# Feed-forward stage: the last layer norm's blocks normalised by ACT with a scale and a shift, the last three blocks added by DVE from PSUM, the last block a store of its own

## The chip, the cores and the metric

The kernel runs on one core of a Trainium2 chip. The metric is the device time of one launch in microseconds. Engines are named as in the profile: PE (TensorE matmuls), PEld (its weight loads), DVE (VectorE), ACT (ScalarE), POOL (GpSimd), SP (SyncE, which issues the DMAs here).

## The reference

Input x is 64 x 64 x 256, so 4096 tokens of 256. Self-attention, cross-attention and a feed-forward part follow one another, each added to x and followed by a layer norm. The change touches the third line only:

```python
def _layernorm(x, axis=-1, eps=1e-05):
    m = jnp.mean(x, axis=axis, keepdims=True)
    v = jnp.var(x, axis=axis, keepdims=True)
    return (x - m) / jnp.sqrt(v + eps)
...
def bitlinear(x, w):
    return jnp.einsum('bsi,oi->bso', _quant_act(x), _quant_weight(w))
gate = jax.nn.sigmoid(bitlinear(x, w_gate))
up = bitlinear(x, w_up)
h = gate * up
return bitlinear(h, w_down)
...
x = _layernorm(x + _L0_attn_ref(x, ...), axis=-1)
x = _layernorm(x + _L0_xattn_ref(x, ctx_2048, ...), axis=-1)
x = _layernorm(x + _L0_ffn_ref(x, L0_ffn_w_gate, L0_ffn_w_up, L0_ffn_w_down), axis=-1)
```

`_quant_act` divides a token's row by its largest magnitude over 127 and rounds; the weights are rounded to -1, 0 and 1 times a scale. The feed-forward width is 1024.

## The kernel before

`build` runs three parts in turn; `feed_forward` is the last. Its first half (lines up to 1116) quantises weights and activations. Its second half is one `nc.Block` in which every engine runs its own instruction list, written out in full without a hardware loop, and semaphores alone tie the lists together. Each engine executes its list strictly in order, so the order in the code is the order on the engine.

The tokens are cut into NB = 32 blocks of 128 rows; X holds all of them in SBUF, 256 columns of f32 for each block. `blocks(slot, lags)` calls `slot(n, has)` for n = 0, 1, 2 ... and `has(k)` says whether block n - k exists. In slot n the engines do, in this order:

- PE: gP(n) and uP(n) (each 4 matmuls of 512 columns, two PSUM banks); dP(n-3), the down projection, 8 matmuls of 256 columns into one of two banks dP0, dP1; hmP(n-2), 8 transposes of hm. gP(n) waits until ACT has read gP(n-1), uP(n) until DVE has read uP(n-1).
- ACT: sig(n), the sigmoid of gP; ds(n-3), dP times its scale; hqT(n-2), which takes the transposed hm from PSUM as bf16.
- DVE: hs(n) = uP times sig; its row maximum and the scales hsc, hinv, dsc; for block n-3 the row statistics (bn_stats at line 1256, bn_aggr at line 1258) of X, which wait for POOL's sum.
- POOL: the sum X = ds + X of block n-3 (line 1212); hm(n) (line 1216), the quantised hs(n), which waits for hinv(n); every fourth slot `roots`, for a group of four blocks: variance + eps (line 1203), then the power -0.5 (line 1205), both on 128 x 4; and the normalise of block n-7 (line 1146), (x - mean) * rstd in place. The roots of group m fall in slot 4m + 7, so in slots 7, 11, ... 31; those of the last group in slot 35.
- SP: one store of four blocks (512 KB) when their normalises are done.

POOL normalises blocks 0 to 27 and DVE, at its end, blocks 28 to 31. Slots 32 to 35 have no sig, hs or hm any more; they are the tail. In the text hs(27) is hs of block 27, and so for the other names.

Of the kernel before, what the change touches and what calls it, by code (L numbers as in the profile page):

```python
# [5 lines left out]
F32 = mybir.dt.float32  # L6
BF16 = mybir.dt.bfloat16
I32 = mybir.dt.int32
ACT = mybir.ActivationFunctionType
AX = mybir.AxisListType.X  # L10

P = 128
B, T, C = 64, 64, 256
# [7 lines left out]
NB = TOK // P  # L21
# [17 lines left out]
def wait(eng, sem, count):  # L39

    if not isinstance(count, int) or count > 0:
        eng.wait_ge(sem, count)
# [486 lines left out]
class Norm:  # L529
# [27 lines left out]
    def roots(self, act):  # L557

        act.wait_ge(self.s_small, 6)
        self.nc.scalar.activation(self.rstd[:, :], self.var[:, :], ACT.Ln, bias=self.eps_col[:, :]).then_inc(self.s_ln, 1)  # L560
        act.wait_ge(self.s_ln, 1)
        self.nc.scalar.activation(self.rstd[:, :], self.rstd[:, :], ACT.Exp, scale=-0.5).then_inc(self.s_rstd, 1)
# [461 lines left out]
def feed_forward(nc, a, X, norm, eps_col, ident, late, out, sem, sb, part):  # L1024
# [100 lines left out]
    hsc, hinv, dsc = sb("hsc", [P, NB], F32), sb("hinv", [P, NB], F32), sb("dsc", [P, NB], F32)  # L1125
    gP, uP, tP = (part.enter_context(nc.psum_tensor(n, [P, DFF], F32)) for n in ("gP", "uP", "hmP"))
    dP = [part.enter_context(nc.psum_tensor(n, [P, TILE], F32)) for n in ("dP0", "dP1")]
    s_g, s_u, s_t, s_dn = (sem("f_" + n) for n in ("g", "u", "t", "dn"))
# [1 line left out]
        "sig", "h", "max", "sc", "inv", "dsc", "hm", "te", "ds", "y"))  # L1130
    s_stats, s_mom, s_rstd, s_normed, s_out = (sem("f_" + n) for n in ("stats", "mom", "rstd", "normed", "out"))
    GROUP = 4
    NG = NB // GROUP
    moments = sb("ln3_moments", [P, NB, 2], F32)
    rstd, power = sb("ln3_rstd", [P, NB], F32), sb("ln3_power", [P, GROUP], F32)
    s_eps, s_power = sem("f_eps"), sem("f_power")

    def blocks(slot, lags):

        for n in range(NB + lags):  # L1140
            slot(n, lambda lag: 0 <= n - lag < NB)

    def normalise(eng, i):

        x = X[:, i, :]
        return eng.tensor_scalar(x, x, moments[:, i, 0:1], rstd[:, i:i + 1], ALU.subtract, ALU.mult)  # L1146

    with nc.Block() as block:  # L1148
        @block.tensor
        def _(pe):  # L1150
            def slot(n, has):
                if has(0):
                    for w, dst, free, ready in ((wg, gP, s_sig, s_g), (wu, uP, s_h, s_u)):
                        wait(pe, free, n)
                        for f in range(DFF // TILE):
                            for c in range(CC):
                                last = nc.tensor.matmul(dst[:, f * TILE:(f + 1) * TILE], xqT[:, c, n * P:(n + 1) * P], w[:, c, f * TILE:(f + 1) * TILE],  # L1157
                                                        start=(c == 0), stop=(c == CC - 1))
                        last.then_inc(ready, 1)
                if has(3):  # L1160
                    e = n - 3
                    wait(pe, s_te, e + 1)
                    wait(pe, s_ds, e - 1)
                    for f in range(FC):
                        last = nc.tensor.matmul(dP[e % 2][:, 0:C], hqT[:, e % 2, f * P:(f + 1) * P], wd[:, f, :], start=(f == 0), stop=(f == FC - 1))
                    last.then_inc(s_dn, 1)
                if has(2):
                    e = n - 2
                    wait(pe, s_hm, e + 1)
                    wait(pe, s_te, e)  # L1170
                    for f in range(FC):
                        last = nc.tensor.transpose(tP[:, f * P:(f + 1) * P], hm[:, e % 2, f * P:(f + 1) * P], ident[:, :])
                    last.then_inc(s_t, 1)

            blocks(slot, 3)

        @block.scalar
        def _(act):
            def slot(n, has):
                if has(0):  # L1180
                    wait(act, s_g, n + 1)
                    wait(act, s_h, n - 1)
                    nc.scalar.activation(sig[:, n % 2, :], gP[:, :], ACT.Sigmoid, scale=gsc[:, n:n + 1]).then_inc(s_sig, 1)
                if has(3):
                    e = n - 3
                    wait(act, s_dn, e + 1)
                    wait(act, s_dsc, e + 1)
                    wait(act, s_y, e - 1)
                    nc.scalar.activation(ds[:, e % 2, :], dP[e % 2][:, 0:C], ACT.Copy, scale=dsc[:, e:e + 1]).then_inc(s_ds, 1)
                if has(2):  # L1190
                    e = n - 2
                    wait(act, s_t, e + 1)
                    wait(act, s_dn, e - 1)
                    nc.scalar.activation(hqT[:, e % 2, :], tP[:, :], ACT.Copy, bias=-MAGIC).then_inc(s_te, 1)

            blocks(slot, 3)

        @block.gpsimd
        def _(pool):
            def roots(m):  # L1200
                own = slice(m * GROUP, (m + 1) * GROUP)
                wait(pool, s_mom, (m + 1) * GROUP)
                nc.gpsimd.tensor_scalar(rstd[:, own], moments[:, own, 1], EPS, None, ALU.add).then_inc(s_eps, 1)  # L1203
                wait(pool, s_eps, m + 1)
                nc.gpsimd.tensor_tensor(rstd[:, own], rstd[:, own], power[:, :], ALU.pow).then_inc(s_rstd, 1)  # L1205

            def slot(n, has):
                if has(3):
                    e = n - 3
                    wait(pool, s_ds, e + 1)  # L1210
                    x = X[:, e, :]
                    nc.gpsimd.tensor_tensor(x, ds[:, e % 2, :], x, ALU.add).then_inc(s_y, 1)  # L1212
                if has(0):
                    wait(pool, s_inv, n + 1)
                    wait(pool, s_t, n - 1)
                    nc.gpsimd.tensor_scalar(hm[:, n % 2, :], hs[:, n % 2, :], hinv[:, n:n + 1], MAGIC, ALU.mult, ALU.add).then_inc(s_hm, 1)  # L1216
                if has(4) and (n - 4) % GROUP == GROUP - 1:
                    roots((n - 4) // GROUP)
                if has(7) and n - 7 < NB - GROUP:
                    e = n - 7  # L1220
                    wait(pool, s_rstd, e // GROUP + 1)
                    normalise(nc.gpsimd, e).then_inc(s_normed, 1)

            nc.gpsimd.memset(power[:, :], -0.5).then_inc(s_power, 1)
            pool.wait_ge(s_power, 1)
            blocks(slot, 4)

        @block.sync
        def _(sp):
            dst = out.rearrange("(n p) c -> p n c", p=P)  # L1230
            for m in range(NG):
                own = slice(m * GROUP, (m + 1) * GROUP)
                sp.wait_ge(s_normed, (m + 1) * GROUP)
                sp.dma_start(dst[:, own, :], X[:, own, :]).then_inc(s_out, 16)
            sp.wait_ge(s_out, 16 * NG)

        @block.vector
        def _(dve):
            def slot(n, has):
                if has(0):  # L1240
                    wait(dve, s_sig, n + 1)
                    wait(dve, s_u, n + 1)
                    wait(dve, s_hm, n - 1)
                    nc.vector.scalar_tensor_tensor(hs[:, n % 2, :], uP[:, :], usc[:, n:n + 1], sig[:, n % 2, :],  # L1244
                                                   ALU.mult, ALU.mult).then_inc(s_h, 1)
                    wait(dve, s_h, n + 1)
                    nc.vector.tensor_reduce(hsc[:, n:n + 1], hs[:, n % 2, :], AX, ALU.max, apply_absolute_value=True).then_inc(s_max, 1)  # L1247
                    wait(dve, s_max, n + 1)
                    nc.vector.tensor_scalar(hsc[:, n:n + 1], hsc[:, n:n + 1], EPS, 1.0 / 127.0, ALU.max, ALU.mult).then_inc(s_sc, 1)  # L1249
                    wait(dve, s_sc, n + 1)  # L1250
                    nc.vector.reciprocal(hinv[:, n:n + 1], hsc[:, n:n + 1]).then_inc(s_inv, 1)  # L1251
                    nc.vector.tensor_scalar(dsc[:, n:n + 1], hsc[:, n:n + 1], wsc[:, 2:3], None, ALU.mult).then_inc(s_dsc, 1)  # L1252
                if has(3):
                    e = n - 3
                    wait(dve, s_y, e + 1)
                    nc.vector.bn_stats(stats[:, e, :], X[:, e, :]).then_inc(s_stats, 1)  # L1256
                    wait(dve, s_stats, e + 1)
                    nc.vector.bn_aggr(moments[:, e, :], stats[:, e, :]).then_inc(s_mom, 1)  # L1258

            blocks(slot, 3)  # L1260
            dve.wait_ge(s_rstd, NG)
            for i in range(NB - GROUP, NB):
                normalise(nc.vector, i).then_inc(s_normed, 1)


def constants():
# [48 lines left out]
```

## Time and profile before

| | us |
|---|---|
| median of the 3 runs | 1627.86 (1627.15 to 1629.86) |
| the profiled execution | 1630.34 |
| its span, first to last instruction | 1628.5 |
| second half of the feed-forward stage, in the span | about 1492 to 1628.5 |

Over the whole span PE is busy 91%, DVE 81%, ACT 82% and POOL 76% of the time, but these are averages over three very different parts. In the last stage the shares must be read from the stage itself. The profile lists instructions with start and duration, and names behind "<-" the instruction whose semaphore ended an engine's idle time. An instruction's own duration may overlap the next one's on the same engine by some hundredths of a microsecond.

### The profile page before, as it was taken

To read this page: it belongs to the slowest core of one execution; us is meant where nothing else is said; L and a number is where in the kernel's file an instruction comes from. 1 tells how busy PE (TensorE), PEld (TensorE's weight loads), DVE (VectorE), ACT (ScalarE), POOL (GpSimd) and SP (SyncE) were. 2 spreads that over 40 slices of the span, in tenths; PEclk is the share of its full clock that TensorE was granted. 3 is DMA by queue.
4 is the path that set the end of the run, shared out by engine and by line. 5 is a ranking of instruction groups with operands and counts; after the bars stand their busy time and mean duration, and the time that the engine had idled before them with its cause. 6 is when DMAs were issued, how large, how long until landed. Compare 5 with 4: busy or idle time off the path is not lost. (4 is left out here: it accounts for less than half of the span.)

```text
span 1628.5 us, 54216 instructions
## 1 busy us (share of the span) xinstructions
PE 1487.4 (91%) x20018; PEld 1083.8 (67%) x20018; DVE 1322.9 (81%) x2913; ACT 1334.4 (82%) x4174; POOL 1231.7 (76%) x1147
## 2 busy tenths in 40 slices
PE   6998999999999999999999968799999999845996
PEld 3666777777777777777777755366666666633664
DVE  3887777777777777777777778699999999967986
ACT  5877888888888888888888856599999999976664
POOL 5999888888898898898898846466666666611787
PEclk9999999999999999999999978999999999976999
DMA  6700000000000000000000002200000000000011
GB/s 222 191 2 15 16 3 15 16 15 3 15 15 3 16 15 5 13 15 15 3 15 3 3 2 68 86 3 2 0 0 0 0 0 0 0 1 0 14 39 53
DMA packets 27066, 36.92 MB, mean 23 GB/s; under 512 B 8288, under 2 KB 19872, under 8 KB 26848
## 3 DMA queue, kind: packets, MB, share of 16 engines
q1 hardware_dynamic: 26848, 33.99, 6.6%
q8 instruction: 140, 2.29, 0.5%
q14 instruction: 78, 0.64, 0.1%
HBM read 29.79 MB, written 4.19 MB: 21 GB/s over the span
## 5 line engine op out<-in xcount | busy, mean ns | idle before, releaser
L420 DVE SCALAR_TENSOR_TENSOR X<-projP,r,X 128x256 f32<-128x256 f32 x512 | 211.3, 476 | 2.5 <-PE projP L254 2.4
L234 PEld LDWEIGHTS svP<-W,xT 128*128 128x128 bf16 x3072 | 182.7, 98 | 31.4 <-issue 1.4
L205 PE MATMUL qkssP<-xT,W 128*128 128x512 bf16 x768 | 190.4, 384 | 13.5 <-POOL W L485 11.1
L480 POOL TENSOR_TENSOR y_sql<-y_sq 128x512 bf16<-128x512 f32 x128 | 133.0, 1039 | 80.5 <-ACT y_sq L321 80.1
L234 PE MATMUL svP<-W,xT 128*128 128x128 bf16 x3072 | 192.9, 219 | 0.7 <-issue 0.7
L205 PE MATMUL kP<-xT,W 128*128 128x512 bf16 x768 | 188.4, 382 | 0.0
L254 PE MATMUL projP<-W,y 128*128 128x256 bf16 x1024 | 177.1, 275 | 3.2 <-POOL yl L480 3.2
L943 ACT ACTIVATE x_probs<-x_scores,x_ntop 128x64 f32<-128x64 f32 x512 | 170.0, 335 | 7.4 <-DVE x_ntop L985 7.4
L336 ACT ACTIVATE probs<-scores,ntop 128x64 f32<-128x64 f32 x512 | 170.5, 339 | 1.9 <-DVE ntop L410 1.9
L1008 POOL TENSOR_TENSOR x_probs<-x_probs,x_inv 128x512 f32<-128x512 f32 x64 | 66.7, 1042 | 107.9 <-DVE x_inv L968 107.9
L480 POOL TENSOR_TENSOR k_sql<-k_sq 128x512 bf16<-128x512 f32 x128 | 133.1, 1040 | 19.8 <-ACT k_sq L341 19.2
L254 PE MATMUL projP<-W,yl 128*128 128x256 bf16 x512 | 140.9, 275 | 0.0
L889 PE MATMUL xq<-qc,WQ 128*128 128x512 bf16 x576 | 136.5, 383 | 3.8 <-PEq L661 2.9
L514 POOL TENSOR_TENSOR ql<-q 128x512 bf16<-128x512 f32 x128 | 139.0, 1086 | 0.0
L480 POOL TENSOR_TENSOR q_sql<-q_sq 128x512 bf16<-128x512 f32 x128 | 133.0, 1039 | 7.6 <-ACT q_sq L328 7.6
L205 PEld LDWEIGHTS kP<-xT,W 128*128 128x128 bf16 x768 | 75.7, 99 | 92.2 <-issue 2.8
L517 POOL TENSOR_TENSOR vl<-v 128x512 bf16<-128x512 f32 x128 | 135.7, 1060 | 0.0
L480 POOL TENSOR_TENSOR yl<-y 128x512 bf16<-128x512 f32 x128 | 133.0, 1039 | 0.0
L450 DVE TENSOR_TENSOR ptl<-pyP,pth 128x256 bf16<-128x256 f32 x128 | 54.3, 424 | 96.8 <-ACT pth L355 96.8
L997 DVE TENSOR_TENSOR qh<-turn 64x512 f32<-64x512 f32 x128 | 128.6, 1005 | 3.1
L1019 POOL TENSOR_TENSOR qhl<-qh 128x1024 bf16<-128x1024 f32 x64 | 121.1, 1893 | 6.2 <-DVE qh L997 6.2
L433 DVE COPY v<-svP 128x512 f32<-128x512 f32 x128 | 88.4, 691 | 44.9 <-PE svP L234 44.1
(190 smaller groups left out, 4829.1 us busy)
## 6 DMA issues: line engine op xcount, KB each, us to landing
w_stage<-in_wqkvp SPq DMA_DIRECT2D x16, 512.0 KB, 3.5
x_stage<-in_xT SPq DMA_DIRECT2D x8, 512.0 KB, 3.6
X<-in_x SPq DMA_DIRECT2D x1, 4096.0 KB, 17.2
x_stage<-in_ctxT SPq DMA_DIRECT2D x8, 512.0 KB, 3.6
out<-X SPq DMA_DIRECT2D x8, 512.0 KB, 2.9
okv<-in_L_xattn_W_o SPq DMA_DIRECT2D x1, 2048.0 KB, 11.7
okv<-in_wgT SPq DMA_DIRECT2D x1, 1024.0 KB, 4.9
okv<-in_wuT SPq DMA_DIRECT2D x1, 1024.0 KB, 7.2
```

What stands on the lines that cost most here:

```text
L205: last = nc.tensor.matmul(dst[:, :], weight(parity, u, i, c), xT[:, z, c, tok], start=(c == 0 and k == 0), stop=(c == CC - 1 and k == 2))
L234: last = nc.tensor.matmul(svP[:, b * D:(b + 1) * D], xT[:, u, c, t * TILE + b * P:t * TILE + (b + 1) * P], weight(parity, z, 2, c), start= ...
L254: last = nc.tensor.matmul(projP[:, b * C:(b + 1) * C], y_part, W[:, (j - 3) // NT % 2, z, 3 * CC * D:], start=(i == 0), stop=(i == 2))
L336: last = nc.scalar.activation(probs[:, b, :], scores[:, b, :], ACT.Exp, bias=ntop[:, b:b + 1], accum_out=total[:, b:b + 1])
L420: last = nc.vector.scalar_tensor_tensor(acc, projP[:, b * C:(b + 1) * C], r[:, PB + b:PB + b + 1], acc, ALU.mult, ALU.add)
L480: return nc.gpsimd.tensor_tensor(dst[:, :], src[:, :], high(src, slice(None), 0, TILE), ALU.subtract)
L514: nc.gpsimd.tensor_tensor(ql[:, j % 2, :], q[:, j % 2, :], high_of(q, j % 2), ALU.subtract).then_inc(s_ql, 1)
L517: nc.gpsimd.tensor_tensor(vl[:, j % 4, :], v[:, j % 4, :], high_of(v, j % 4), ALU.subtract).then_inc(s_vl, 1)
L889: last = nc.tensor.matmul(qP[k][:, :], at(WQ[:, u, :, k], g), qc[:, z, j * TILE:(j + 1) * TILE], start=(i == 0), stop=(i == 2))
L943: last = nc.scalar.activation(probs[:, s, b, :], scores[:, b, :], ACT.Exp, bias=ntop[:, b:b + 1], accum_out=total[:, b:b + 1])
L997: last = nc.vector.tensor_tensor(qh[KVC:P, j % 2, :, i, :], turn[rows, 0], turn[rows, 1], ALU.add)
L1019: nc.gpsimd.tensor_tensor(qhl[:, s, :], flat, flat.bitcast(BF16)[:, 1::2], ALU.subtract).then_inc(s_ql, 1)
```

## The change

ACT normalises blocks 0 to 27 in place of POOL, as Identity(x * rstd + shift) with shift = -mean * rstd; block n-8 is done in slot n, behind hqT(n-2). POOL's `roots` computes shift for these seven groups with two more instructions. Blocks from LATE = 29 on are summed by DVE directly from PSUM, X = dP * dsc + X, so ACT's ds and POOL's sum are left out for them. The last group of four is split in a group of three (28 to 30) and one of one (31), each with roots and a store of its own; DVE normalises them as before. PE's wait before dP follows the new readers of dP. Stores of the first 28 blocks wait for ACT.

```diff
     GROUP = 4
-    NG = NB // GROUP
+    groups = [slice(i, i + GROUP) for i in range(0, NB - GROUP, GROUP)] + [slice(NB - GROUP, NB - 1), slice(NB - 1, NB)]
+    NG, MAIN, LATE = len(groups), NB - GROUP, NB - 3
...
 (PE)
-                    wait(pe, s_ds, e - 1)
+                    wait(pe, s_ds, min(e - 1, LATE))
+                    wait(pe, s_y, e - 1 if e - 2 >= LATE else 0)
...
 (ACT)
-                if has(3):
+                if has(3) and n - 3 < LATE:
                     e = n - 3
...
-            blocks(slot, 3)
+                if has(8) and n - 8 < MAIN:
+                    e = n - 8
+                    x = X[:, e, :]
+                    wait(act, s_shift, e // GROUP + 1)
+                    nc.scalar.activation(x, x, ACT.Identity, bias=shift[:, e:e + 1], scale=rstd[:, e:e + 1]).then_inc(s_by_act, 1)
+
+            blocks(slot, 4)
...
 (POOL)
             def roots(m):
-                own = slice(m * GROUP, (m + 1) * GROUP)
-                wait(pool, s_mom, (m + 1) * GROUP)
+                own = groups[m]
+                wait(pool, s_mom, own.stop)
                 nc.gpsimd.tensor_scalar(rstd[:, own], moments[:, own, 1], EPS, None, ALU.add).then_inc(s_eps, 1)
                 wait(pool, s_eps, m + 1)
-                nc.gpsimd.tensor_tensor(rstd[:, own], rstd[:, own], power[:, :], ALU.pow).then_inc(s_rstd, 1)
+                nc.gpsimd.tensor_tensor(rstd[:, own], rstd[:, own], power[:, 0:own.stop - own.start], ALU.pow).then_inc(s_rstd, 1)
+                if own.stop <= MAIN:
+                    nc.gpsimd.tensor_scalar(shift[:, own], moments[:, own, 0], -1.0, None, ALU.mult).then_inc(s_neg, 1)
+                    wait(pool, s_neg, m + 1)
+                    wait(pool, s_rstd, m + 1)
+                    nc.gpsimd.tensor_tensor(shift[:, own], shift[:, own], rstd[:, own], ALU.mult).then_inc(s_shift, 1)
...
-                if has(4) and (n - 4) % GROUP == GROUP - 1:
-                    roots((n - 4) // GROUP)
-                if has(7) and n - 7 < NB - GROUP:
-                    e = n - 7
-                    wait(pool, s_rstd, e // GROUP + 1)
-                    normalise(nc.gpsimd, e).then_inc(s_normed, 1)
+                for m in range(NG):
+                    if n - 4 == groups[m].stop - 1:
+                        roots(m)
...
 (DVE)
                 if has(3):
                     e = n - 3
+                    if e >= LATE:
+                        x = X[:, e, :]
+                        wait(dve, s_dn, e + 1)
+                        wait(dve, s_dsc, e + 1)
+                        wait(dve, s_y, e)
+                        nc.vector.scalar_tensor_tensor(x, dP[e % 2][:, 0:C], dsc[:, e:e + 1], x, ALU.mult, ALU.add).then_inc(s_y, 1)
                     wait(dve, s_y, e + 1)
                     nc.vector.bn_stats(stats[:, e, :], X[:, e, :]).then_inc(s_stats, 1)
```

On POOL, from the roots in slot 27 to hm in slot 28. Before:

```order
L1203 TENSOR_SCALAR ln3_rstd<-ln3_moments 128x4 [waits f_mom]
L1205 TENSOR_TENSOR ln3_rstd<-ln3_rstd,ln3_power 128x4 [waits f_eps]
L1146 TENSOR_SCALAR X<-X,ln3_moments,ln3_rstd 128x256 [waits f_rstd]
L1212 TENSOR_TENSOR X<-ds,X 128x256 [waits f_ds]
L1216 TENSOR_SCALAR hm<-hs,hinv 128x1024 [waits f_t,f_inv]
```

After:

```order
L1206 TENSOR_SCALAR ln3_rstd<-ln3_moments 128x4 [waits f_mom]
L1208 TENSOR_TENSOR ln3_rstd<-ln3_rstd,ln3_power 128x4 [waits f_eps]
L1210 TENSOR_SCALAR ln3_shift<-ln3_moments 128x4
L1213 TENSOR_TENSOR ln3_shift<-ln3_shift,ln3_rstd 128x4 [waits f_rstd,f_neg]
L1220 TENSOR_TENSOR X<-ds,X 128x256 [waits f_ds]
L1224 TENSOR_SCALAR hm<-hs,hinv 128x1024 [waits f_t,f_inv]
```

The normalise between the roots and the next sum is gone; two instructions on 128 x 4 stand in its place.

On ACT, slot 28 and the start of slot 29: sig(28), ds(25), hqT(26), sig(29), ds(26). Before:

```order
L1183 ACTIVATE sig<-gP,gsc 128x1024 [waits f_h,f_g]
L1189 ACTIVATE ds<-dP1,dsc 128x256 [waits f_y,f_dsc,f_dn]
L1194 ACTIVATE hqT<-hmP 128x1024 [waits f_dn,f_t]
L1183 ACTIVATE sig<-gP,gsc 128x1024 [waits f_h,f_g]
L1189 ACTIVATE ds<-dP0,dsc 128x256 [waits f_y,f_dsc,f_dn]
```

After:

```order
L1181 ACTIVATE sig<-gP,gsc 128x1024 [waits f_h,f_g]
L1187 ACTIVATE ds<-dP1,dsc 128x256 [waits f_y,f_dsc,f_dn]
L1192 ACTIVATE hqT<-hmP 128x1024 [waits f_dn,f_t]
L1197 ACTIVATE X<-X,ln3_shift,ln3_rstd 128x256 [waits f_shift]
L1181 ACTIVATE sig<-gP,gsc 128x1024 [waits f_h,f_g]
L1187 ACTIVATE ds<-dP0,dsc 128x256 [waits f_y,f_dsc,f_dn]
```

A normalise with a wait for shift stands between hqT and the next block's sig.

On DVE, the end of its list, from the statistics of block 31. Before:

```order
L1256 BN_STATS ln3_stats<-X 128x6 [waits f_y]
L1258 BN_AGGR ln3_moments<-ln3_stats 128x2 [waits f_stats]
L1146 TENSOR_SCALAR X<-X,ln3_moments,ln3_rstd 128x256 [waits f_rstd]
L1146 TENSOR_SCALAR X<-X,ln3_moments,ln3_rstd 128x256 x3
L1148 UNCONDITIONAL_BRANCH
```

After:

```order
L1267 SCALAR_TENSOR_TENSOR X<-dP1,dsc,X 128x256 [waits f_y,f_dsc,f_dn]
L1269 BN_STATS ln3_stats<-X 128x6 [waits f_y]
L1271 BN_AGGR ln3_moments<-ln3_stats 128x2 [waits f_stats]
L1279 TENSOR_SCALAR X<-X,ln3_moments,ln3_rstd 128x256 [waits f_rstd]
L1279 TENSOR_SCALAR X<-X,ln3_moments,ln3_rstd 128x256 x2
L1279 TENSOR_SCALAR X<-X,ln3_moments,ln3_rstd 128x256 [waits f_rstd]
```

DVE makes the sum of block 31 itself, and the wait for the last roots stands before its last normalise alone.

## Rows read from the trace of the kernel before

**Rows 1.** Who waited for instructions on ds, last stage: us, times.

```profile
  DVE ln_stats L1256: 13.1, 9
```

**Rows 2.** Timeline: start, us, engine, line, operation; DVE and POOL, blocks 27 to 29.

```profile
1594.61 1.28 DVE L1244 SCALAR_TENSOR_TENSOR hs<-uP,usc,sig 128x1024 f32<-128x1024 f32 x1
...
1597.37 0.16 DVE L1251 RECIPROCAL hinv<-hsc 128x1 f32<-128x1 f32 x1
...
1597.64 1.12 POOL L1216 TENSOR_SCALAR hm<-hs,hinv 128x1024 f32<-128x1024 f32 x1 [0.50 <-DVE hinv L1251]
...
1598.13 1.28 DVE L1244 SCALAR_TENSOR_TENSOR hs<-uP,usc,sig 128x1024 f32<-128x1024 f32 x1
...
1598.85 0.23 POOL L1203 TENSOR_SCALAR ln_rstd<-ln_moments 128x4 f32<-128x4 f32 x1
1599.16 1.04 POOL L1205 TENSOR_TENSOR ln_rstd<-ln_rstd,ln_power 128x4 f32<-128x4 f32 x1
...
1600.31 1.22 POOL L1146 TENSOR_SCALAR X<-X,ln_moments,ln_rstd 128x256 f32<-128x256 f32 x1
...
1601.50 0.73 POOL L1212 TENSOR_TENSOR X<-ds,X 128x256 f32<-128x256 f32 x1
...
1602.26 0.43 DVE L1256 BATCH_NORM_STATS2 ln_stats<-X 128x6 f32<-128x256 f32 x1 [1.10 <-POOL X L1212]
...
1602.83 1.28 DVE L1244 SCALAR_TENSOR_TENSOR hs<-uP,usc,sig 128x1024 f32<-128x1024 f32 x1
```

**Rows 3.** Timeline of the same stretch, PE and ACT: hmP(27), ds(25), hqT(26), sig(29).

```profile
1597.70 1.04 PE L1172 MATMUL hmP<-ident,hm 128*128 128x128 f32 x8
1597.90 0.47 ACT L1189 ACTIVATE ds<-dP,dsc 128x256 f32<-128x256 f32 x1 [0.61 <-PE dP L1165]
...
1598.78 1.02 ACT L1194 ACTIVATE hqT<-hmP 128x1024 bf16<-128x1024 f32 x1 [0.40 <-PE hmP L1172]
...
1599.70 1.11 ACT L1183 ACTIVATE sig<-gP,gsc 128x1024 f32<-128x1024 f32 x1
```

**Rows 4.** Timeline of the tail, from hm(31) to the last normalises.

```profile
1612.88 1.12 POOL L1216 TENSOR_SCALAR hm<-hs,hinv 128x1024 f32<-128x1024 f32 x1 [0.50 <-DVE hinv L1251]
...
1616.58 1.02 ACT L1194 ACTIVATE hqT<-hmP 128x1024 bf16<-128x1024 f32 x1 [0.40 <-PE hmP L1172]
...
1617.49 0.43 DVE L1256 BATCH_NORM_STATS2 ln_stats<-X 128x6 f32<-128x256 f32 x1 [4.04 <-POOL X L1212]
...
1617.65 1.05 PE L1165 MATMUL dP<-wd,hqT 128*128 128x256 bf16 x8 [1.11 <-ACT hqT L1194]
...
1621.23 1.22 POOL L1146 TENSOR_SCALAR X<-X,ln_moments,ln_rstd 128x256 f32<-128x256 f32 x1
1621.28 0.43 DVE L1256 BATCH_NORM_STATS2 ln_stats<-X 128x6 f32<-128x256 f32 x1 [1.25 <-POOL X L1212]
1621.74 0.18 DVE L1258 BATCH_NORM_AGGREGATE ln_moments<-ln_stats 128x2 f32<-128x6 f32 x1
...
1622.73 1.04 POOL L1205 TENSOR_TENSOR ln_rstd<-ln_rstd,ln_power 128x4 f32<-128x4 f32 x1
1623.80 1.38 DVE L1146 TENSOR_SCALAR X<-X,ln_moments,ln_rstd 128x256 f32<-128x256 f32 x4 [1.89 <-POOL ln_rstd L1205]
```

**Rows 5.** Groups of instructions over the whole span: busy us, mean ns, then idle before.

```profile
L420 DVE SCALAR_TENSOR_TENSOR X<-projP,r,X 128x256 f32<-128x256 f32 x512 | 211.3, 476 | 2.5 <-PE projP L254 2.4
...
L1063 ACT ACTIVATE xs<-X,magic,xinv 128x256 f32<-128x256 f32 x32 | 16.6, 588 | 5.1 <-DVE xinv L1091 5.1
...
L1055 ACT ACT_TABLE_LOAD x1 | 1.3, 1283 | 0.0
...
L813 POOL TENSOR_TENSOR kvw<-kvf,kvw 128x128 bf16<-128x128 f32 x1 | 0.5, 473 | 0.0
```

**Rows 6.** DMA issues: count, KB each, median us from issue to landing.

```profile
out<-X SPq DMA_DIRECT2D x8, 512.0 KB, 2.9
...
tabs<-in_rope SPq DMA_DIRECT2D x1, 96.0 KB, 2.1
```

More of the change, by code:

```diff
@@ L1132, in feed_forward @@
     GROUP = 4
-    NG = NB // GROUP
+    groups = [slice(i, i + GROUP) for i in range(0, NB - GROUP, GROUP)] + [slice(NB - GROUP, NB - 1), slice(NB - 1, NB)]
+    NG, MAIN, LATE = len(groups), NB - GROUP, NB - 3
     moments = sb("ln3_moments", [P, NB, 2], F32)
-    rstd, power = sb("ln3_rstd", [P, NB], F32), sb("ln3_power", [P, GROUP], F32)
-    s_eps, s_power = sem("f_eps"), sem("f_power")
+    rstd, shift, power = sb("ln3_rstd", [P, NB], F32), sb("ln3_shift", [P, NB], F32), sb("ln3_power", [P, GROUP], F32)
+    s_eps, s_power, s_neg, s_shift = sem("f_eps"), sem("f_power"), sem("f_neg"), sem("f_shift")
+    s_by_act = sem("f_byact")
     def blocks(slot, lags):
@@ L1141, in blocks @@
             slot(n, lambda lag: 0 <= n - lag < NB)
-    def normalise(eng, i):
-        x = X[:, i, :]
-        return eng.tensor_scalar(x, x, moments[:, i, 0:1], rstd[:, i:i + 1], ALU.subtract, ALU.mult)
     with nc.Block() as block:
@@ L1200, in roots @@
             def roots(m):
-                own = slice(m * GROUP, (m + 1) * GROUP)
-                wait(pool, s_mom, (m + 1) * GROUP)
+                own = groups[m]
+                wait(pool, s_mom, own.stop)
                 nc.gpsimd.tensor_scalar(rstd[:, own], moments[:, own, 1], EPS, None, ALU.add).then_inc(s_eps, 1)
                 wait(pool, s_eps, m + 1)
-                nc.gpsimd.tensor_tensor(rstd[:, own], rstd[:, own], power[:, :], ALU.pow).then_inc(s_rstd, 1)
+                nc.gpsimd.tensor_tensor(rstd[:, own], rstd[:, own], power[:, 0:own.stop - own.start], ALU.pow).then_inc(s_rstd, 1)
[4 more added lines that the diff above has]
+                    nc.gpsimd.tensor_tensor(shift[:, own], shift[:, own], rstd[:, own], ALU.mult).then_inc(s_shift, 1)
             def slot(n, has):
-                if has(3):
+                if has(3) and n - 3 < LATE:
                     e = n - 3
@@ L1230, in _ @@
             dst = out.rearrange("(n p) c -> p n c", p=P)
-            for m in range(NG):
-                own = slice(m * GROUP, (m + 1) * GROUP)
-                sp.wait_ge(s_normed, (m + 1) * GROUP)
+            for own in groups:
+                if own.stop <= MAIN:
+                    sp.wait_ge(s_by_act, own.stop)
+                else:
+                    sp.wait_ge(s_normed, own.stop - MAIN)
                 sp.dma_start(dst[:, own, :], X[:, own, :]).then_inc(s_out, 16)
@@ L1260, in _ @@
             blocks(slot, 3)
-            dve.wait_ge(s_rstd, NG)
-            for i in range(NB - GROUP, NB):
-                normalise(nc.vector, i).then_inc(s_normed, 1)
+            for m in (NG - 2, NG - 1):
+                own = groups[m]
+                dve.wait_ge(s_rstd, m + 1)
+                for i in range(own.start, own.stop):
+                    x = X[:, i, :]
+                    nc.vector.tensor_scalar(x, x, moments[:, i, 0:1], rstd[:, i:i + 1], ALU.subtract, ALU.mult).then_inc(s_normed, 1)
 def constants():
```

## Prediction, made before the changed kernel was run

> **What bounds the kernel now.** I read four views of the profile, in this order: what the row statistics wait for, the instructions of one group of four blocks in order of time, the same for the last microseconds, and the prices of like operations. Only the last stage matters: it is the only one the change touches.
>
> Call slot n the one in which DVE makes hs(n). In a plain slot DVE is never idle: hs(27) starts at 1594.61 and hs(28) at 1598.13, 3.52 us later [rows 2], with the block's maximum, scales and row statistics between them. In one slot of four it stops. POOL finishes hm(27), then computes the roots (0.23, then the power, 1.04), then normalises a block (1.22), and only then adds block 25 (0.73), for whose sum DVE's statistics have waited 1.10 us. So hs(29) starts at 1602.83, 4.70 us after hs(28) [rows 2]. DVE's statistics wait nine times and 13.1 us in all [rows 1]. Three of these waits lie in the tail (4.04, and twice 1.25, [rows 4]); the other 6.6 us are six waits of 1.1, one for each of the roots in slots 7, 11, ... 27. Since DVE has no slack in a plain slot, each is paid in full: 4.70 - 3.52 = 1.18 us.
>
> The tail is bound elsewhere. TensorE ends dP(31) at 1618.70, but POOL is busy with an add and a normalise for each leftover block; it starts the last normalise at 1621.23, the last power ends at 1623.77, and DVE then normalises four blocks to 1625.18 [rows 4]. The 512 KB store of these four lands 2.9 us later [rows 6], and the span ends at 1628.5: 3.32 us after the last normalise.
>
> **The six groups.** POOL loses its 28 normalises of 1.22 and gains, per group, a negation and a product on 128x4. The negation is of the form of the 0.233 us step in [rows 2]. A product of 128x4 is not in the trace. The nearest rows: two tensor-tensor operations, 473 ns at 128 elements [rows 5] and 0.73 us at 256 [rows 2], whose straight line gives 0.23 at four; and the power on the same 128x4, 1.04. I take 0.23, since a product is like the plain operations and not like a power; 1.04 stays as the upper bound.
>
> ACT gains 24 normalises inside its loop (and four in the tail). The row with the same form, f32 128x256 from SBUF with a bias and a scale per partition, is 588 ns [rows 5]. In a plain slot this hides. After hs(27), with start t = 1594.61: the transposes hmP start at t + 3.09 and end at t + 4.13, hqT runs from t + 4.17 to t + 5.19 [rows 3]; consecutive ACT instructions overlap by 0.10 (hqT ends at 1599.80, sig starts at 1599.70). So the normalise starts at t + 5.09 and sig(29) at t + 5.58; it ends 1.11 later, at t + 6.69, and hs(29) is due at t + 7.03. The cover is 0.34 less a handover, which I take as 0.06 (between 0.03, power to DVE at the end, and 0.11, hinv to hm, [rows 2, 4]): **0.28 us of slack**. If that cover were gone, each 0.1 of excess would cost 0.05 a slot, because the loop spans two slots. ACT's 0.47 us ds [rows 3] starts when dP ends, so it is not pushed.
>
> In the slot after the roots it does not hide. ACT takes its instructions in order, and the normalise of the new group's first block now stands ahead of sig(29) and waits for shift. In the times of rows 2 and 3: the power ends at 1600.20; negation to 1600.43; product (0.08 later, as between the 128x4 step and the power) 1600.51 to 1600.74; normalise(20) on ACT 1600.80 to 1601.39, though ACT was free at 1599.80; sig(29) 1601.29 to 1602.40; hs(29) at 1602.46. It was 1602.83, and undisturbed it would be 1598.13 + 3.52 = 1601.65. So the stall shrinks only from 1.18 to 0.81: **0.37 us a group, 2.2 us for six**. The old wait, by itself, would shrink more: the add of block 25 runs from 1600.77 to 1601.50 and the statistics start at 1601.53 and not 1602.26, 0.73 earlier. ACT's wait is what comes in its place and ends last. Behind it are queued sig(29), for which DVE waits, and with it gP of block 30 on TensorE. gP(30) needs the PSUM that sig(29) reads and moves with it; uP(30) waits for the end of hs(29) anyway, and TensorE is not asked for hs(30) before that, so nothing is added.
>
> **The tail**, in the times of before. hm(31) still starts at 1612.88. Its roots give shift 3.10 later (1600.74 - 1597.64), at 1615.98; normalise(24) runs on ACT from 1616.04 to 1616.63, and hqT(31), which starts at 1616.58 now [rows 4], can start 0.10 before that ends. A tie: no cost, but no cover either. dP(31) ends at 1618.70 as before. ACT's ds and POOL's add for blocks 29 to 31 are gone; DVE's one operation from PSUM has the form of the 476 ns row [rows 5]: 1618.74 to 1619.22. Statistics 1619.25, aggregation 0.46 later (1621.28 to 1621.74, [rows 4]) and ended at 1619.89. POOL is idle: first step at 1620.00, power at 1620.31 to 1621.35 (I take 1.04 for one element as for four). DVE has by then normalised blocks 28 to 30, whose roots needed dP(30) only; the last block takes 0.41 (1.38 for four back to back is 0.345 each, a lone one is a little longer): 1621.38 to 1621.79, against 1625.18. **3.4 us.**
>
> The last store is 128 KB and not 512. The nearest row is a 96 KB transfer landing in 2.1 us, against 2.9 [rows 6]. I take 2.1, so the span ends 2.5 and not 3.3 us after the normalise: **0.8 us**, between 0 (no gain by size) and 1.1. The 384 KB store ahead of it on SP's queue is issued at about 1621.0 and would be nearly through.
>
> The Trainium skill, "DMA: Bandwidth & Descriptors", section on the anatomy of one DMA, gives about 2.0 us plus bytes over 436 GB/s. By it, as an estimate, the last store would take 2.3 us in place of 3.2, a gain of 0.9 and not 0.8. Its figure for 512 KB is 0.3 above this trace's 2.9, so the row decides, and the sum moves by 0.1 us.
>
> Sum: 2.2 + 3.4 + 0.8 = 6.4 us. The profiled execution took 1630.34 with a span of 1628.5, so it would become 1623.9 with a span of 1622.1. It lay 2.5 us above the median of the runs shown. From that median, 1627.86, the forecast is **1621.5 us**.
>
> **Rivals.**
>
> *ACT's wait hides.* If shift came earlier than I think or sig had more room, each group would gain the 0.73 of POOL's path: 4.4 in place of 2.2, and 1619.3 us. Against it: ACT is free at 1599.80 and shift can't be there before the power ends at 1600.20. For it: only the overlap assumptions at each handover. 12%.
>
> *The product costs what the power costs.* With 1.04 us in place of 0.23 each group stalls 1.62 and not 0.81, a loss of 0.44 a group against now, 2.6 for six; the same 0.8 then holds hqT(31) in the tail, 4.2 less 0.8 is 3.4. Net gain 0.8 us: 1627.1. For it: all other small POOL tensor-tensor rows here are this power. 13%.
>
> *The last store or the last roots give nothing.* The tail gains only 3.4 or less (store lands in 2.9, or a wait on the small roots), total about 5: 1622.9. 15%.
>
> *Slower: ACT becomes the bound.* One mechanism, in its loop hqT, normalise, sig: if the normalise took more than 0.59 + 0.28 = 0.87 us, plain slots would lengthen too. Up to there 0.1 us costs 0.7 (six groups and the tail), so 6.4 falls to 4.4; beyond it 1.6 per 0.1 (18 plain slots by 0.05 more). Break-even is at 1.15 us, 3.3 us slower at 1.35. At POOL's price for this very operation, 1.22 [rows 2], it gives 1.2 us slower, 1629.1; at 1.5, about 1633.5. For it: ACT's added work is the only one in every slot, and the operands are its own output area, f32 in place. Against: the 588 ns row has the same shape and operands. Nor is a table exchanged: the 588 ns operations run behind the load at L1055 [rows 5], and Sigmoid after them without another. 5% in all, most of it at or above 1.2.
>
> *The forecast*: 55%.
>
> **Numbers.** A measurement of this kernel can tell some 0.2%, 3.3 us, from no change. The forecast, the hidden wait and the weak store are all faster by more than that: 82%. The slow product, and milder cases of ACT's, lie within it: 14%. Slower: 4%. The range covers the hidden wait (1619.3 less the spread of the base, about 1) and reaches up to 1625.3, past the point (1624.3) where a product with half the extra would land; left out are the slow product in full and ACT's case, some 18%.
>
> **What would show it.** Right: hs starts 3.52 apart in three slots and about 4.3 in the fourth; ahead of ACT's normalise, once in four, an idle time of about 1.0 us ended by POOL's product; DVE's statistics waiting some 0.4 in that slot, with the rest of the stall ahead of hs and ended by sig; ACT's normalise near 590 ns; POOL's product near 230 ns; from the end of dP(31) to the end of the last normalise 3.1 us, where it was 6.5; three stores in the last nine microseconds, the last landing in 2.1. Wrong: hs waiting for sig in plain slots (ACT's loop is too long), hqT(31) waiting behind normalise(24) (shift late), or the last power starting later than 2 us after dP(31).

## The result, and the profile after

| | before | after |
|---|---|---|
| median, us (11 runs each) | 1628.44 | 1623.43 |
| ratio, 95% interval | | 0.9963 (0.9950 to 0.9976) |
| span of the profiled execution | 1628.5 | 1618.4 |
| hs(0) to hs(31) in the profile | 114.34 | 112.19 |
| hs(31) to the end of the span | 18.65 | 14.35 |

The ratio is worth 6.0 us, at a forecast of 6.4 (1621.5 from 1627.86, a ratio of 0.9961); its interval spans 3.9 to 8.1 us, so the whole times alone don't tell the forecast from a gain of 5. The median after, 1623.43, lies 1.9 above the 1621.5 and below the 1625.3 up to which the forecast reached; that of before is itself 0.6 above the 1627.86 that the forecast started from. The two spans differ by 10.1 us, which is more than the change did: 3.65 of it had arisen before hs(0), in stages that are the same in both kernels. The two distances in the last rows of the table leave that out, and all runs below are read by them. They give 2.15 + 4.30 = 6.45 us. One row of each kernel carries the start of both:

```profile
L1244 DVE SCALAR_TENSOR_TENSOR hs<-uP,usc,sig x32: 1273/1284/1286, 1495.5 to 1609.9; 128x1024 f32<-128x1024 f32 x32
```

is hs before (shortest, median and longest duration in ns, then the first and the last start), and after the change:

```profile
L1251 DVE SCALAR_TENSOR_TENSOR hs<-uP,usc,sig x32: 1273/1284/1286, 1491.9 to 1604.0; 128x1024 f32<-128x1024 f32 x32
```

The slot after the roots, as [rows 2] and [rows 3] showed it before: timeline of the changed kernel (start, us, engine, line, operation, and the idle time before it with what ended it).

```profile
1592.19 1.12 POOL L1224 TENSOR_SCALAR hm<-hs,hinv 128x1024 f32<-128x1024 f32 x1 [1.71 <-DVE hinv L1258]
...
1592.68 1.28 DVE L1251 SCALAR_TENSOR_TENSOR hs<-uP,usc,sig 128x1024 f32<-128x1024 f32 x1
...
1593.71 1.03 POOL L1208 TENSOR_TENSOR ln_rstd<-ln_rstd,ln_power 128x4 f32<-128x4 f32 x1
...
1594.83 0.24 POOL L1210 TENSOR_SCALAR ln_shift<-ln_moments 128x4 f32<-128x4 f32 x1
...
1595.15 0.20 POOL L1213 TENSOR_TENSOR ln_shift<-ln_shift,ln_rstd 128x4 f32<-128x4 f32 x1
...
1595.39 0.60 ACT L1197 ACTIVATE X<-X,ln_shift,ln_rstd 128x256 f32<-128x256 f32 x1 [1.03 <-POOL ln_shift L1213]
...
1595.89 1.09 ACT L1181 ACTIVATE sig<-gP,gsc 128x1024 f32<-128x1024 f32 x1
...
1596.07 0.43 DVE L1269 BATCH_NORM_STATS2 ln_stats<-X 128x6 f32<-128x256 f32 x1 [0.35 <-POOL X L1220]
...
1597.02 1.28 DVE L1251 SCALAR_TENSOR_TENSOR hs<-uP,usc,sig 128x1024 f32<-128x1024 f32 x1 [0.31 <-ACT sig L1181]
```

hs(28) to hs(29) is 4.34 us, where it was 4.70. DVE waits twice: 0.35 for POOL's sum, then 0.31 for sig, which stands on ACT behind a normalise that waited 1.03 for shift. The rest of the 0.83 by which this pitch exceeds the plain 3.51 is overlap lost at the two waits: in a plain slot the statistics and hs each start some 0.08 before the instruction ahead of them has ended. POOL, without its normalise, now waits 1.7 us for hinv in a plain slot (first row), where it waited 0.50. The waits of the whole stage, us in total, times and longest:

```profile
ACT X L1197 <- POOL ln_shift L1213: 7.4, 7, 1.5
...
DVE ln_stats L1269 <- POOL X L1220: 2.1, 6, 0.4
DVE hs L1251 <- ACT sig L1181: 1.9, 6, 0.3
```

Before, [rows 1] had one line of 13.1 us in their place, of which 6.6 lay in the six groups. The tail, for [rows 4]:

```profile
1610.26 0.60 ACT L1197 ACTIVATE X<-X,ln_shift,ln_rstd 128x256 f32<-128x256 f32 x1 [1.50 <-POOL ln_shift L1213]
...
1610.77 1.02 ACT L1192 ACTIVATE hqT<-hmP 128x1024 bf16<-128x1024 f32 x1
...
1611.85 1.05 PE L1163 MATMUL dP<-wd,hqT 128*128 128x256 bf16 x8 [1.11 <-ACT hqT L1192]
1612.93 0.48 DVE L1267 SCALAR_TENSOR_TENSOR X<-dP,dsc,X 128x256 f32<-128x256 f32 x1 [1.87 <-PE dP L1163]
1613.45 0.43 DVE L1269 BATCH_NORM_STATS2 ln_stats<-X 128x6 f32<-128x256 f32 x1
...
1614.01 1.58 DVE L1279 TENSOR_SCALAR X<-X,ln_moments,ln_rstd 128x256 f32<-128x256 f32 x4
...
1614.57 0.58 POOL L1208 TENSOR_TENSOR ln_rstd<-ln_rstd,ln_power 128x1 f32<-128x1 f32 x1
```

From the start of dP(31) to the last normalise's end (1614.01 + 1.58 = 1615.59) it takes 3.74 us; before, 1617.65 to 1625.18, it took 7.53. The last stores, for [rows 6] (count, KB, us to landing):

```profile
out<-X SPq DMA_DIRECT2D x7, 512.0 KB, 2.9
out<-X SPq DMA_DIRECT2D x1, 384.0 KB, 2.5
out<-X SPq DMA_DIRECT2D x1, 128.0 KB, 2.4
```

### The profile page after: what moved, and what is told of

Its sections match the earlier page's. It is cut to its first block and busy times, and to the rows that moved or that the text cites. A ratio compares the mean times of both kernels' runs of the same rounds, so it can differ in the third digit from the quotient of the medians.

```text
span 1618.4 us, 54034 instructions
## 1 busy us (share of the span) xinstructions
PE 1459.8 (90%) x19815; PEld 1082.1 (67%) x20018; DVE 1322.4 (82%) x2916; ACT 1345.4 (83%) x4199; POOL 1201.4 (74%) x1132
## 5 line engine op out<-in xcount | busy, mean ns | idle before, releaser
L205 PE MATMUL qkssP<-xT,W 128*128 128x512 bf16 x641 | 161.3, 382 | 33.5 <-issue 20.3
L889 PE MATMUL xq<-qc,WQ 128*128 128x512 bf16 x514 | 123.0, 382 | 7.4 <-PEq L661 3.1
```

The lines of the kernel that those rows point to most:

```text
L205: last = nc.tensor.matmul(dst[:, :], weight(parity, u, i, c), xT[:, z, c, tok], start=(c == 0 and k == 0), stop=(c == CC - 1 and k == 2))
L889: last = nc.tensor.matmul(qP[k][:, :], at(WQ[:, u, :, k], g), qc[:, z, j * TILE:(j + 1) * TILE], start=(i == 0), stop=(i == 2))
```

## The experiments

Every kernel is the changed one with the edit shown. "First" is hs(0) to hs(31), "tail" is hs(31) to the end of the span, both in us and from one profiled execution of each kernel; kernels that don't differ in the first distance repeat it to 0.05 us (112.19 to 112.24). Each ratio is taken against runs of the kernel before from the same series. The last three kernels ran once.

| kernel | first | tail | ratio to before (95%) |
|---|---|---|---|
| before | 114.34 | 18.65 | |
| after | 112.19 | 14.35 | 0.9963 (0.9950 to 0.9976) |
| ACT's normalise only | 112.24 | 17.45 | 0.9963 (0.9943 to 0.9984) |
| new tail only | 114.44 | 16.59 | 0.9970 (0.9951 to 0.9988) |
| ACT's normalise one slot later | 109.89 | 14.54 | 0.9939 (0.9922 to 0.9956) |
| roots one slot later | 116.52 | 14.32 | 0.9982 (0.9962 to 1.0002) |
| second power | 118.11 | 15.30 | 1.0006 (0.9991 to 1.0021) |
| roots ahead of hm | 107.26 | 14.29 | 0.9933 (0.9908 to 0.9958) |
| POOL normalises, roots ahead of hm | 110.52 | 16.20 | 0.9967 (0.9943 to 0.9991) |
| one last store | 112.21 | 16.21 | one run |
| no sums on DVE | 112.19 | 16.45 | one run |
| the same, roots of 28 to 30 first | 112.21 | 15.94 | one run |

### The two halves of the change

New tail only: POOL normalises as before.

```diff
 (ACT)
-                if has(8) and n - 8 < MAIN:
-                    e = n - 8
-                    ...
-            blocks(slot, 4)
+            blocks(slot, 3)
 (POOL, behind the roots; no shift is computed)
+                if has(7) and n - 7 < MAIN:
+                    e = n - 7
+                    x = X[:, e, :]
+                    wait(pool, s_rstd, e // GROUP + 1)
+                    nc.gpsimd.tensor_scalar(x, x, moments[:, e, 0:1], rstd[:, e:e + 1], ALU.subtract, ALU.mult).then_inc(s_by_act, 1)
```

> The new tail alone: POOL normalises blocks 0 to 27 as before the change, with no shift, while DVE makes the last three sums and the last store is split. hs(0) to hs(31) as before the change, 114.3 us. Tail: if its 4.3 us came from the new sums and stores alone, 14.35; Theory A expects less, because POOL still has four normalises of 1.22 to do behind hm(31) and between the last two roots, so the last power ends about 1.8 us later than with ACT's normalise: about 16.0 to 16.3.

ACT's normalise only: one group of four at the end, no sums on DVE.

```diff
-    groups = [slice(i, i + GROUP) for i in range(0, NB - GROUP, GROUP)] + [slice(NB - GROUP, NB - 1), slice(NB - 1, NB)]
-    NG, MAIN, LATE = len(groups), NB - GROUP, NB - 3
+    groups = [slice(i, i + GROUP) for i in range(0, NB, GROUP)]
+    NG, MAIN, LATE = len(groups), NB - GROUP, NB
...
-            for m in (NG - 2, NG - 1):
+            for m in (NG - 1,):
```

> ACT's normalise alone; the last three blocks go through ACT and POOL as before the change, one group of four and one store at the end. hs(0) to hs(31) 112.2 us as after the change. Tail: ds(30) and hqT(31) stand behind the normalise that waits for shift (0.4 us), then ds 0.47 and POOL's sum 0.73, roots of four, four normalises and a 512 KB store: 18.65 - 1.2 = about 17.4 us. If taking the normalise off POOL did nothing for the tail: 18.65.

Measured: 114.44 and 16.59 for the new tail, 112.24 and 17.45 for ACT's normalise. So the 2.1 us of the first distance come from ACT's normalise alone. In the tail the parts give 2.06 and 1.20 each on its own, but 4.30 where both are made: they need each other. Without ACT's normalise POOL's four leftover normalises hold the last roots back; with POOL free, ACT's and POOL's detour for the last sums does (the run with no sums on DVE, below, has 16.45 where the change has 14.35). In the timeline of the new tail alone POOL is still at its last normalise when the sums are long done:

```profile
1616.00 3.64 POOL L1227 TENSOR_SCALAR X<-X,ln_moments,ln_rstd 128x256 f32<-128x256 f32 x3
...
1620.17 0.18 DVE L1271 BATCH_NORM_AGGREGATE ln_moments<-ln_stats 128x2 f32<-128x6 f32 x1
1620.81 1.27 POOL L1227 TENSOR_SCALAR X<-X,ln_moments,ln_rstd 128x256 f32<-128x256 f32 x1
...
1622.40 0.58 POOL L1203 TENSOR_TENSOR ln_rstd<-ln_rstd,ln_power 128x1 f32<-128x1 f32 x1
1623.02 0.41 DVE L1279 TENSOR_SCALAR X<-X,ln_moments,ln_rstd 128x256 f32<-128x256 f32 x1 [0.80 <-POOL ln_rstd L1203]
```

The excess over 16.0 to 16.3 is in the store: SP issues the last three within 1.4 us there (2.3 after the change), and the last one lands in 3.1 us and not 2.4.

### Which wait ends last in a group

Two waits stand in the slot after the roots, so two edits take one away each. ACT's normalise one slot later:

```diff
-                if has(8) and n - 8 < MAIN:
-                    e = n - 8
+                if has(9) and n - 9 < MAIN:
+                    e = n - 9
...
-            blocks(slot, 4)
+            blocks(slot, 5)
```

> ACT's normalise one slot later (block n-9). Two distances are read from the trace: from the start of hs(0) to the start of hs(31), 114.3 us before and 112.2 after the change, and from hs(31) to the end of the span, 18.65 and 14.35. Theory A (ACT's wait for shift ends last in each group): with the wait covered, the stall of a group falls from 0.82 to about 0.44, what POOL's late sum leaves, so the first distance becomes 109.9 us; DVE still waits 0.35 for POOL's sum, six times. Rival B (the stall is POOL's sum alone, ACT's wait lies beside it): 112.2, unchanged. Both expect the tail at about 14.4.

Roots one slot later, behind the sum, which frees the sum and delays shift:

```diff
+                for m in range(NG):
+                    if n - (5 if groups[m].stop <= MAIN else 4) == groups[m].stop - 1:
+                        roots(m)
                 if has(0):
                     wait(pool, s_inv, n + 1)
...
-                for m in range(NG):
-                    if n - 4 == groups[m].stop - 1:
-                        roots(m)
```

> The roots of the first seven groups run one slot later, behind the sum and ahead of hm. DVE's statistics then never wait for POOL's sum, but shift comes 0.73 us later for ACT. Theory A: the stall of a group grows from 0.82 to 1.55, hs(0) to hs(31) becomes 116.6 us, slower than before the change. Rival B (POOL's sum is the stall): the stall goes, 112.2 - 6 x 0.82 = 107.3 us. Tail unchanged for both, about 14.4.

Measured: 109.89 and 116.52 us, against 109.9 and 116.6 for theory A (ACT's wait for shift ends last). Its rival (POOL's sum alone) expected 112.2 and 107.3. With the normalise one slot later ACT's wait for shift is gone from the list and DVE's for the sum stays, at its old size (0.35 of a stall that is now 0.44):

```profile
DVE ln_stats L1269 <- POOL X L1220: 2.1, 6, 0.4
```

With the roots one slot later it is the other way round, and the remaining wait is the longer one:

```profile
ACT X L1197 <- POOL ln_shift L1213: 11.7, 7, 1.7
...
DVE hs L1251 <- ACT sig L1181: 8.9, 6, 1.6
```

### More of the same wait

A power more on 128x4, ahead of the negation; its result is overwritten:

```diff
                 if own.stop <= MAIN:
+                    nc.gpsimd.tensor_tensor(shift[:, own], moments[:, own, 1], power[:, :], ALU.pow).then_inc(s_spare, 1)
+                    wait(pool, s_spare, m + 1)
```

> A second power on 128x4, whose result is not used, stands ahead of the negation in the roots of the first seven groups: about 1.12 us later shift and sum. Theory A (ACT's wait on the path, nothing hides it): the stall of a group grows by the full 1.12, from 0.82 to 1.94; hs(0) to hs(31) 112.2 + 6.7 = 118.9 us; tail longer by 1.1, since norm(24) holds hqT(31): 15.5. If there was room beside the stall: less than 0.5 a group, under 115.

Measured: 118.11 and 15.30; each stall is 1.82 us, 0.99 longer than after the change. The extra power costs 1.00 and not 1.12, because it follows the first without a wait and starts as that one ends:

```profile
1597.38 1.03 POOL L1208 TENSOR_TENSOR ln_rstd<-ln_rstd,ln_power 128x4 f32<-128x4 f32 x1
...
1598.38 1.01 POOL L1210 TENSOR_TENSOR ln_shift<-ln_moments,ln_power 128x4 f32<-128x4 f32 x1
```

So what shift is late by is paid in full in the groups and nearly so in the tail (0.95 of 1.00), and the time is that of the kernel before (1.0006). This also prices the slow-product rival: a product of power's cost would have eaten nearly all of the gain.

### Taking both waits away

Roots in the same slot, behind the sum but ahead of hm:

```diff
+                for m in range(NG):
+                    if n - 4 == groups[m].stop - 1:
+                        roots(m)
                 if has(0):
                     wait(pool, s_inv, n + 1)
...
-                for m in range(NG):
-                    if n - 4 == groups[m].stop - 1:
-                        roots(m)
```

> The roots stay in their slot but run ahead of hm, behind the sum. Theory A: shift is ready before ACT asks for it and POOL's next sum is in time, so both waits of a group go; hs(0) to hs(31) 112.2 - 6 x 0.82 = 107.3 us, and no idle time of DVE in any slot after the first; hm of that slot comes about 0.4 us later, which nobody waits for. Rival C (a late hm is paid: DVE's scales or the transposes of hm wait for it): 0.4 us a group come back, 109.7 us or more. Tail 14.4 for both, with norm(24) no longer waiting. In all 4.9 us faster than after the change, about 0.66% faster than before it; by C 3.4 us or less.

Measured: 107.26 and 14.29, as theory A said, and a ratio of 0.9933. This is the fastest kernel here, 5.0 us below the change in the two distances together (4.93 + 0.06); the intervals of the two ratios overlap, so the distances decide. POOL had been idle 1.7 us in each slot, waiting for hinv; the roots now run in that time. In its timeline hm(27) starts without a wait at 1589.10, some 0.3 us late (hinv(27) ended at 1588.69, and in a plain slot hm follows it by 0.1), and nobody waits for it: its transposes run a slot later, at 1592.36.

```profile
1587.48 1.03 POOL L1208 TENSOR_TENSOR ln_rstd<-ln_rstd,ln_power 128x4 f32<-128x4 f32 x1
...
1588.92 0.20 POOL L1213 TENSOR_TENSOR ln_shift<-ln_shift,ln_rstd 128x4 f32<-128x4 f32 x1
...
1589.10 1.12 POOL L1227 TENSOR_SCALAR hm<-hs,hinv 128x1024 f32<-128x1024 f32 x1
1589.16 0.18 DVE L1271 BATCH_NORM_AGGREGATE ln_moments<-ln_stats 128x2 f32<-128x6 f32 x1
1589.27 1.28 DVE L1251 SCALAR_TENSOR_TENSOR hs<-uP,usc,sig 128x1024 f32<-128x1024 f32 x1
...
1592.36 1.04 PE L1170 MATMUL hmP<-ident,hm 128*128 128x128 f32 x8
```

Is ACT needed for that at all? POOL normalises as before the change, with the new tail, and the roots stand ahead of hm (the edit of "new tail only" and the one above, together):

> POOL still normalises blocks 0 to 27 (the new tail, no shift), but its roots run ahead of hm in their slot. If what cost the stall was the roots' place in POOL's list, moving them does part of the work without ACT: roots 1.36 from the end of the sum, hm 1.12, normalise 1.22, so the next sum ends about 0.6 late against 1.18 before: hs(0) to hs(31) 114.3 - 6 x 0.6 = 110.8 us, shorter than after the change (112.2). If POOL's load (sum, hm, normalise: 3.1 of each 3.5 us, plus 1.4 for four blocks) is the limit wherever the roots stand: 114.3, unchanged.

Measured: 110.52 us in the first distance, shorter than after the change (112.19), with no work moved to ACT. Five stalls of 0.67 remain, and none for the first group, whose roots meet a POOL that has no normalises yet:

```profile
DVE ln_stats L1269 <- POOL X L1215: 2.9, 5, 0.6
```

So the place of the roots cost more than the normalise did; but sum, hm and normalise take 3.07 us of a slot of 3.51, and the roots need 0.23 + 1.04 = 1.27 more in one slot, so a stall stays. The tail is 16.20, and first distance and tail add up to 126.72, against 126.54 after the change: beside the new tail, moving the roots alone comes within 0.2 us of moving the normalises alone. ACT's normalise is worth 110.52 - 107.26 = 3.26 us once the roots stand right, and 2.25 (114.44 - 112.19) where they stand wrong.

### The parts of the tail

One last store: the edits to `groups` and to DVE's last loop of "ACT's normalise only", with LATE kept.

> Only the split of the last group is undone: DVE still makes the last three sums, but roots for four blocks run after the last statistics, and one store of 512 KB ends the kernel. hs(0) to hs(31) unchanged, 112.2 us. Tail: the power on 128x4 instead of 128x1 (1.04 against 0.58, 0.46), four normalises instead of one behind it (1.38 against 0.40, about 1.0), and the larger store (3.3 against 2.8 to the end of the span, 0.5): 14.35 + 1.95 = 16.3 us. If the split was worth only the store: 14.9.

Measured: 16.21. The split is worth 1.86 us, most of it not the store itself but the roots and normalises behind the last statistics: the last normalise ends 12.90 us after hs(31) and not 11.54 (1.36), and from there to the end of the span it takes 3.31 and not 2.81 (0.50).

No sums on DVE:

```diff
-    NG, MAIN, LATE = len(groups), NB - GROUP, NB - 3
+    NG, MAIN, LATE = len(groups), NB - GROUP, NB
```

> Only DVE's sums from PSUM are undone: the last three blocks go through ACT's scaled copy and POOL's sum, with the split groups kept. hs(0) to hs(31) unchanged, 112.2 us. Tail: ds 0.47 and sum 0.73 with two handovers in place of 0.48 (0.8 us), and ds(30) now stands between norm(24), which waits for shift, and hqT(31) (about 0.4): 14.35 + 1.2 = 15.6 us. If ACT's order there cost nothing: 15.15.

Measured: 16.45, and the expectation missed by 0.85. Its timeline shows what it had left out:

```profile
1615.32 0.72 POOL L1220 TENSOR_TENSOR X<-ds,X 128x256 f32<-128x256 f32 x1 [1.80 <-ACT ds L1187]
...
1616.45 0.87 POOL L1208 TENSOR_TENSOR ln_rstd<-ln_rstd,ln_power 128x3 f32<-128x3 f32 x1
...
1617.31 0.23 POOL L1206 TENSOR_SCALAR ln_rstd<-ln_moments 128x1 f32<-128x1 f32 x1
1617.37 1.38 DVE L1279 TENSOR_SCALAR X<-X,ln_moments,ln_rstd 128x256 f32<-128x256 f32 x4 [0.64 <-POOL ln_rstd L1208]
```

The roots of blocks 28 to 30 stand on POOL behind the sum of block 31, which waits for the last ds, although their statistics were done 1.9 us earlier (1614.20). DVE's first three normalises wait for them, and so does the last root. With these roots moved ahead of that sum:

```diff
+                if n == NB + 2:
+                    roots(NG - 2)
                 if has(3) and n - 3 < LATE:
...
-                for m in range(NG):
+                for m in range(NG - 2):
                     if n - 4 == groups[m].stop - 1:
                         roots(m)
+                if n == NB + 3:
+                    roots(NG - 1)
```

> As the run without DVE's sums (tail 16.45 us, 0.85 over its expectation), with one step moved: in slot 34 POOL computes the roots of blocks 28 to 30 ahead of the sum of block 31. If the 0.85 was POOL's order (these roots behind that sum, the last roots behind both, and DVE's four normalises behind the first): tail about 15.6 us. If it was something in ACT's or DVE's sums themselves: 16.4, unchanged. hs(0) to hs(31) 112.2 for both.

Measured: 15.94, so 0.51 of the 0.85 was that order. From hs(31) to the last normalise's end it is now 12.82 us (1605.67 to 1618.49), 1.28 more than after the change (1604.05 to 1615.59, 11.54): the 1.2 expected. The other 0.3 lie behind that end, 3.11 us to the end of the span against 2.81. They are not in the last store, which lands in 2.4 us in both. SP's last two waits in this run are

```profile
SPq L1145 <- DMA out<-X: 2.0, 1, 2.0
SPq L1145 <- PEq L1145: 0.5, 1, 0.5
```

The first, for the last landing, is 2.0 us after the change too; the second is 0.2 there:

```profile
SPq L1145 <- PEq L1145: 0.2, 1, 0.2
```

The run with no sums on DVE has the same 0.5. The profile puts this wait down to PE's queue, though PE's last matmul ended more than 6 us earlier; what it stands for is open.

## Why the prediction was right

**What bounds the stage.** Six stalls of 1.18 us and a tail bound by POOL: the first held exactly (from the fourth block on the pitches of hs are 3.50 to 3.52 in plain slots and 4.70 or 4.71 in the others). For the second stand the two halves: taking the normalises off POOL gives the tail 1.20 us by itself and 2.24 on top of the new tail (16.59 to 14.35).

**ACT's normalise hides in plain slots.** It costs 595 ns (588 forecast), and no plain slot with row statistics became longer in any run (3.50 to 3.52). The cover was put at 0.28 us; no run tested where it ends.

**ACT's wait takes the place of the one removed.** Forecast: ACT idle about 1.0, DVE's statistics 0.4, hs(28) to hs(29) 4.33, a stall of 0.81. Measured: 1.03, 0.35, 4.34 and 0.83. The two one-sided runs show that it is this wait that ends last. The gain of 2.2 us came out as 2.15, and the rival in which it hides (1619.3 us) is what the run with the normalise one slot later brought about by its edit: 4.45 us in the first distance, where the rival had 4.4.

**The product of 128x4.** Taken at 0.23 between 0.23 and 1.04; it is 0.20.

**The tail.** hqT(31) behind normalise(24) was called a tie without cover. Measured in both kernels from the start of hs(31), hqT(31) starts at 6.72 after the change and 6.73 before. Two terms were off and nearly cancelled, so that their sum fits within 0.1 us is luck. To the last normalise's end the gain was 15.33 - 11.54 = 3.79 and not 3.4: the power on one element takes 0.58 and not 1.04, so from the end of dP(31) to that of the last normalise there are 2.69 us and not the 3.1 of the forecast. Behind it the gain was 3.32 - 2.81 = 0.51 and not 0.8: the 128 KB store lands in 2.4 and not in 2.1. Sum 4.30, against 4.2. The 2.1 came from a row that reads 96 KB into SBUF, while this is a store. The Trainium skill ("DMA: Bandwidth & Descriptors", section "Anatomy of one DMA — SWDGE (gpsimd) path") fits about 2.0 us plus the bytes over 436 GB/s to DMAs issued from GpSimd. By that, as an estimate, 128 KB take 2.3 us, near the 2.4 here, where SP issues the store; for 512 KB it gives 3.2, and this trace has 2.9 in every run, so it doesn't fit these stores throughout.

**What the prediction did not see.** It treated the roots' place as given. The slack it needed, POOL's wait for hinv, grows from 0.50 us [rows 2] to 1.7 by the very move it was costing, and 4.9 us lay in using it.

## What to carry to other kernels

When work moves to an engine that executes in order, ask what each of its instructions waits for and what stands behind it: a normalise of 0.6 us that hid completely in plain slots cost 0.38 us a group (112.19 against 109.89, six groups) where its operand was late; the other 0.44 of the stall were POOL's late sum. A wait that occurs once in several iterations is priced in the iteration after its cause, by the chain from the late result to the next instruction of the saturated engine; take the first producer in that chain out of the way before moving work elsewhere. Short steps that nobody needs soon belong into the producer's idle time, here ahead of the instruction that waits.

## What the runs showed of the hardware

The power on POOL takes longer with more elements per partition: 1.04 us for 128x4, 0.87 for 128x3, 0.58 for 128x1, where the addition on 128x4 takes 0.23, the one on 128x1 0.23 to 0.30, and the product 0.20.

Between kernels whose code is the same up to there the start of hs(0) varied from 1490.6 to 1501.9 us (before: 1495.5; the second power: 1490.6; ACT's normalise only: 1501.9), while the first distance repeated within 0.1 us between kernels that don't differ in it (112.19, 112.24, 112.21, 112.19, 112.21). So a change of some microseconds in the last stage is measured far more closely by the distance between two marks in one profile than by the whole span. The latest starts (1501.9, 1499.4 and 1495.9) belong to the lowest mean granted clocks of TensorE (0.965, 0.966 and 0.967), the three earliest (1490.6 to 1491.7) to the highest (0.973); where in the earlier stages the difference arises was not followed up.
